# First four slots of an AdaLN and expert kernel written out, two pairs of blocks turned by TensorE, scatters set one by one among GpSimd's other work, and the last two pairs' scatters spaced by landings

## The reference, cut to what matters

```python
z = relu(hidden @ Wd[profile] + bd)              # 16 blocks of 256 rows x 256, a profile of 8 for each block
y = hidden + z @ Wu[profile] + bu
y = layernorm(y) * g[profile] + b[profile]
probs = softmax(y @ gate_w + gate_b)             # 8 experts
values, experts = top_k(probs, 2); values /= sum(values) + 1e-9
shared = gelu(y @ sh_w1 + sh_b1) @ sh_w2 + sh_b2                 # 256 -> 1024 -> 256
moe = sum over the two experts e of value_e * (gelu(y @ ew1[e] + eb1[e]) @ ew2[e] + eb2[e])
out = x + (y + shared + moe)
```

## Time and profile before

| | |
|---|---|
| median of 3 runs | 654.41 us (653.47 to 654.74) |
| the profiled execution's own time | 652.95 us, span 650.9 us |
| PE busy | 599.8 us, 92% of the span |
| DVE, ACT, POOL busy | 77%, 60%, 63% |
| first shared product / first expert product | 39.80 us / 243.46 us |

### The profile page before, as it was taken

One profiled execution on the slowest core, in us unless ns is written; L12 is line 12 of the kernel. 1 busy time (PEld: TensorE's weight loads), 2 busy tenths in 40 slices (PEclk: granted clock), 3 DMA queues, 4 the chain that ended last, 5 costly groups with the idle time before them and its releaser, 6 DMA issues.

```text
span 650.9 us, 16857 instructions
## 1 busy us (share of the span) xinstructions
PE 599.8 (92%) x5073; PEld 484.5 (74%) x5073; DVE 503.1 (77%) x1198; ACT 389.3 (60%) x662; POOL 413.1 (63%) x320
## 2 busy tenths in 40 slices
PE   4356999999989899999999999999999999999994
PEld 2223666766646668888888888888888888889883
DVE  3859889979975793898989898988896665656883
ACT  1638666667767774667675858576754444434641
POOL 2435687788887601285959585858688575756743
PEclk9768999999989999999999999999999999999998
DMA  7964467666144756367657585666686342424410
GB/s 265 304 145 133 128 190 151 215 195 154 57 126 121 247 160 191 84 125 134 147 105 155 126 142 130 137 133 129 90 71 73 52 73 44 67 41 59 69 26 3
DMA packets 116740, 81.31 MB, mean 125 GB/s; under 512 B 71090, under 2 KB 106162, under 8 KB 116658
## 3 DMA queue, kind: packets, MB, share of 16 engines
q1 hardware_dynamic: 101346, 61.16, 38.4%
q0 software_dynamic: 13296, 16.92, 15.3%
q10 hardware_dynamic: 2016, 2.16, 1.1%
HBM read 43.21 MB, written 24.42 MB: 104 GB/s over the span
## 4 chain that ended last, share of the span: by engine, by line
PE 71%; DVE 9%; issue 7%; POOL 4%; ACT 3%; DMA 3%; SPq 2%; POOLq 0%; ACTq 0%; DVEq 0%
PE H L1219 29%; PE Y L1235 29%; PE Y L1170 6%; PE H L1158 6%; SPq L287 2%; POOL xs_rows L430 2%; DVE wreg L768 1%; DMA xT<-wreg 1%; POOL wreg L413 1%; DVE wreg L737 1%; DMA wreg<-in_wpack 1%; DVE wreg L734 1%; DVE wreg L828 1%; ACT hf L554 1%; ACT wreg L501 1%
## 5 line engine op out<-in xcount | busy, mean ns | idle before, releaser
L608 ACT ACTIVATE hf<-H,prme 128x256 f32<-128x256 f32 (+1 forms) x312 | 151.0, 541 | 112.1 <-issue 97.4
L1219 PE MATMUL H<-xT,wreg 128*128 128x256 f16 (+1 forms) x1872 | 200.4, 263 | 0.2
L1235 PE MATMUL Y<-wreg,hh 128*128 x1136 | 188.6, 273 | 3.6 <-issue 2.4
L1219 PEld LDWEIGHTS H<-xT,wreg 128*128 x1872 | 171.9, 98 | 21.1 <-issue 0.7
L1235 PE MATMUL Y<-wreg,hl 128*128 x568 | 154.8, 273 | 0.0
L1235 PEld LDWEIGHTS Y<-wreg,hh 128*128 128x128 f16 x1136 | 111.0, 98 | 20.6 <-issue 6.1
L1031 DVE SCALAR_TENSOR_TENSOR hl<-hf,prme,hh 128x512 f16<-128x512 f32 (+1 forms) x156 | 115.1, 738 | 5.6
L1029 DVE TENSOR_SCALAR hh<-hf,prme 128x512 f16<-128x512 f32 (+1 forms) x156 | 84.6, 542 | 40.4 <-ACT hf L608 38.3
L457 POOL TENSOR_SCALAR b2w<-b2t,wsel 128x256 f32<-128x256 f32 x71 | 99.1, 1606 | 23.6 <-DMA b2t<-in_b 18.1
L1158 PE MATMUL H<-xT,wreg 128*128 128x512 f16 x384 | 93.8, 396 | 11.8 <-DMA xT<-wreg 11.7
L468 POOL DMA_INDIRECT out_y<-hh,xgm x36 | 64.7, 1799 | 58.0 <-DVE hh L1057 38.9
(11 more groups left out here) (189 smaller groups left out, 672.9 us busy)
## 6 DMA issues: line engine op xcount, KB each, us to landing
stage<-in_w SPq DMA_DIRECT2D x16, 1024.0 KB
b2t<-in_b SPq DMA_DIRECT2D x39, 128.0 KB
wreg<-in_wpack SPq DMA_DIRECT2D x16, 256.5 KB
wreg<-in_xt SPq DMA_DIRECT2D x16, 256.0 KB
wreg<-in_x SPq DMA_DIRECT2D x16, 256.0 KB, 5.6
wreg<-in_vecs SPq DMA_DIRECT2D x16, 256.0 KB, 4.0
out_y<-wreg SPq DMA_DIRECT2D x16, 256.0 KB, 2.2
xs_rows<-wreg SPq DMA_DIRECT2D x9, 260.0 KB
```

The costliest lines, as they stand in the source:

```text
L608: act.activation(hf[:, c, half * w:(half + 1) * w], H[c][:, half * w:(half + 1) * w], ACT.Gelu_apprx_tanh, bias=pr[:, ch:ch + 1], scale=pr ...
L1219: m = pe.matmul(H[c][:, half * w:(half + 1) * w], we[:, bass.ds(e + h * 2048 + k * 1024 + col, P)], xp[:, a + k, 0:w], start=i == 0, stop= ...
L1235: m = pe.matmul(Y[n % 2][:, j * D:(j + 1) * D], hx[:, n % 2, c * w + j * P:c * w + (j + 1) * P], we[:, bass.ds(e + 4096 + h * 2048 + c * D ...
```

## The change

Four things are done. **First slots.** Slots -7 to -1 leave the loops: each engine has their steps as straight code in another order, with other banks of PSUM for the first products (`z_of`, `u_of`, `MX0`), root and norm of pair 0 done block by block, and loads of more blocks started ahead. ScalarE's queue starts the 1 MB of unit 0 ahead of the four small vectors and takes over x of blocks 0 and 1. VectorE's `constants` stand ahead of the `v_xs` chain; `gate_halves`, the second block of pair 1 and unit 1 move behind slot 0. **Turning.** Pairs 0 and 1 (`PT` = 2) are turned by TensorE (`turn`, float32 products with the identity) into Y0 and Y1, and split from there by `high_turned` (ScalarE) and `low_turned` (VectorE). SP starts no transposes for them. **Zeros in waits.** `warm(n)` multiplies n times zeros by zeros, 14 times at the start and 6 times ahead of `turn(0)`. **Scatters.** Of pairs 0 to 5 single scatters stand between other GpSimd instructions. In pairs 6 and 7 each group of two waits until the group before it has landed.

```diff
+def turns(p):
+    return 16 * 4 * len(range(p % 3 + (3 if p % 3 < PT else 0), p + 1, 3))
...
+            load_shared(0)
             for dst, src in ((gnb_t[:, :], gnb.rearrange("t e (a c) -> (t e a) c", c=32)),
...
-            load_shared(0)
+            for b in range(2):
+                act.dma_start(acc_of(b), x[b].rearrange("(j p) d -> p j d", p=P)).then_inc(d_x[b], 16)
...
+            unit_sums(0)
+            relu(0)
+            relu(1)
+            load_shared(1)
+            unit_high(0)
+            relu(2)
+            norm(0, 0, 2)
+            norm(0, 2, 4)
+            high_turned(0)
+            high_turned(1)
+            relu(3)
+            high_rows(0)
+            unit_sums(1)
...
+            def turn(b):
+                pe.wait_ge(q_xn, b + 1)
...
+                for k in range(2):
+                    for j in range(2):
+                        t = pe.matmul(tn_of(b)[:, k, j * P:(j + 1) * P], yb_of(b)[:, j * D + k * P:j * D + (k + 1) * P], ident[:, :], start=True, stop=True)
+                t.then_inc(p_tn, 1)
...
+            def high_turned(b):
+                act.wait_ge(p_tn, b + 1)
+                act.wait_ge(v_xs, 1)
+                act.activation(xT16_of(b // 2)[:, 0:2, cols_of(b)], tn_of(b), ACT.Copy, scale=XS).then_inc(a_xt, 1)
...
+            def low_turned(b):
+                dve.wait_ge(a_xt, b + 1)
+                xp = xT16_of(b // 2)
+                dve.scalar_tensor_tensor(xp[:, 2:4, cols_of(b)], tn_of(b), XS, xp[:, 0:2, cols_of(b)], ALU.mult, ALU.subtract).then_inc(v_xt, 1)
...
+            def warm(n):
+                for i in range(n):
+                    pe.matmul(H[0][:, :], zpad[:, 0, 0:P], zpad[:, 0, 0:512], start=True, stop=True)
...
-                if c == 0:
-                    pe.wait_ge(d_tr[t % 3], 16 * 4 * (t // 3 + 1))
-                    if t == 0:
-                        pe.wait_ge(v_low, 1)
+                if c == 0 and t < PT:
+                    pe.wait_ge(v_xt, 2 * t + 2)
+                elif c == 0:
+                    pe.wait_ge(d_tr[t % 3], turns(t))
...
+            def scatter(p, i, q):
+                if (i, q) == (0, 0):
...
+                if p >= NP - 2 and q == 0 and i:
+                    pool.wait_ge(d_row[p % 3], 16 * (8 * (p // 3) + 2 * i))
+                elif p == NP - 2 and q == 0:
+                    pool.wait_ge(d_row[(p - 1) % 3], 16 * (8 * ((p - 1) // 3) + 7))
+                elif p == NP - 1 and q == 0:
+                    pool.wait_ge(d_row[(p - 1) % 3], 16 * 8 * ((p - 1) // 3 + 1))
```

More of the change, by code:

```diff
@@ L51 @@
 EARLY = 4
-START = [-6, -2, 27, 27]
+PT = 2
 PACE = 6
@@ L63, in upto, with seen @@
     return sum(blocks(k) for k in range(n))
-def early(s, d):
-    return [u for u in range(EARLY) if s == START[u] + d]
+def seen(p, hi):
+    return p + 1 + (p > 0 or hi == 4)
+def turns(p):
+    return 16 * 4 * len(range(p % 3 + (3 if p % 3 < PT else 0), p + 1, 3))
 def late(n, c, d):
@@ L339, in sync_program @@
             load_x(3)
-            for s in range(FIRST, NS):
+            load_xT(3)
+            load_adapter(3)
+            load_gb(2)
+            load_gb(3)
+            load_x(4)
+            load_x(5)
+            load_xT(4)
+            load_adapter(4)
+            load_xT(5)
+            load_adapter(5)
+            load_gb(4)
+            load_gb(5)
+            for s in range(NS):
                 if s == 26:
@@ L349, in sync_program @@
                 for p in at(s, -2):
[L350 to L353, removed]
+                    load_x(2 * p)
+                    load_x(2 * p + 1)
+                    for b in range(2 * p, 2 * p + 2):
                         load_xT(b)
@@ new lines, in even, with odd @@
+            def even(s, o, i, q):
+                for p in at(s, o):
+                    if p % 2 == 0 and p < NP - 2:
+                        scatter(p, i, q)
+            def odd(s, o, i, q):
+                for p in at(s, o):
+                    if p % 2 and p < NP - 2:
+                        scatter(p, i, q)
+            xb(0)
+            xb(1)
+            root(0, 0, 2)
+            root(0, 2, 4)
+            rows(0)
+            rows(1)
+            xb(2)
+            xb(3)
+            root(1)
@@ L974, in shared_rows @@
                 dve.scalar_tensor_tensor(a, Y[b % 2][:, :], pr[:, 10:11], a, ALU.mult, ALU.add).then_inc(v_acc, 1)
-            for s in range(FIRST, NS):
+            unit_scale(0)
+            variances(0, statistics(0), 0, 2)
+            variances(0, statistics(1), 2, 4)
+            roots(0, 0, 2)
+            roots(0, 2, 4)
+            gain(0)
+            gain(1)
+            unit_low(0)
+            low_turned(0)
+            low_turned(1)
+            statistics(2)
+            variances(1, statistics(3))
+            low_rows(0)
+            for s in range(NS):
                 t, q = s // 4, s % 4
@@ L997, in vector_program @@
                     choose(p)
-                if s == -1:
-                    gate_halves()
-                    constants()
-                if s < 4:
-                    for u in early(s, 4):
-                        unit_low(u)
-                if s < 4:
-                    for u in early(s, 2):
-                        unit_scale(u)
+                if s == 1:
+                    unit_scale(1)
                 if s == 28:
                     unit_scale(2)
-                if s >= 0:
-                    low_h(t, q)
+                low_h(t, q)
+                if s == 0:
+                    gate_halves()
+                if s == 2:
+                    low_turned(2)
+                    low_turned(3)
+                    unit_low(1)
                 if s == 27:
```

235 lines of the change are left out of this document (150 added, 85 removed).

## The result

The changed kernel takes **669.43 us** (median of 4 runs, 669.11 to 669.59); the kernel before, beside it, 654.4. The ratio is 1.0231 with a 95% interval of 1.0214 to 1.0249. The forecast was 643.3, so it was wrong by 26 us and in sign.

A forecast was written before the change was run, and what follows sets the result against it. TensorE was taken as short of work before 65 us and nearly full after. Start -9.6, single scatters -4.9 and spaced scatters +3.4 sum to -11.1, from 654.41 to 643.3 us; range 637 to 650.

The forecast's parts named there:

- the 14.5 gained ahead: Before the hand-over to the experts: gains of 9.6 us from the start and 4.9 from single scatters.
- The start: Up to the first `gemm2`: slot 0 11.6 us earlier, 2.0 given back, gain 9.6, between -1.7 and 16.2.
- Steps 1 and 2: Start: small vectors land at 9.5, 3.9 us late; the `v_xs` chain with `constants` then ends at 14.4.
- Step 3: Start: `unit_scale(0)`, statistics, root, norm and `gain` end at 23.7, the adapter's products fitting beside them.
- Step 4: Start: `unit_low(0)` takes 3.0 us and hides the turning; after two `low_turned` of 0.75 each, slot 0 starts at 28.2.
- given back in slots 0 to 3: VectorE's 7.4 us of moved work mostly fits 8.9 us of idle time; charged 2.0, between 0 and 7.4.
- Rival B: Late small vectors and work moved into slots 0 to 3 leave 4 to 5 of 9.6; 648 to 649; chance 0.17.
- D: VectorE's chain takes the start's gain, TensorE waiting at slots 5 to 22; about 654 us; chance 0.05.
- Single scatters: Scatters between GpSimd's instructions free VectorE; `low_rows(6)` 3.1 us earlier against slot 21; gain 4.9, bounds nothing to 5.8.
- Spaced scatters: Pairs 6 and 7: eight groups of 2.24 us plus landings of 2.76 delay the asking for rows; loss 3.4.
- Rival C: Spaced scatters take over the hand-over, landings of 5.6 us losing 26.1, deciding from 4.2; 666.0 us; chance 0.08.
- What the text said would show it wrong: Slot 0 after 33, the wait before slot 22 remaining, or the first expert product waiting over 5 us for rows.

The follow-up runs named there:

- e3: The changed kernel without the landing waits and with `gate_halves` between the two `low_turned` of the start; 658.28 us, ratio 1.0042 to the kernel before.
- e5: The changed kernel without landing waits, scatters of pairs 0 to 5 in runs as before, `gate_halves` between the two `low_turned`; 649.87 us, ratio 0.9924 to the kernel before.
- e9: e7 with `residual(0)`, `residual(1)` and `tokens(0)` ahead of `root(1)` in GpSimd's start; 646.84 us, ratio 0.99 to the kernel before.
- e6: The kernel before with only the scatters of pairs 0 to 5 placed singly, as in the changed kernel; 658.62 us, ratio 1.0062.
- e8: The same kernel as e4, run once more on another chip; 650.16 us in one execution.
- e2: The kernel before with only the landing waits added, pair 6's first waiting for all of pair 5; 669.38 us, ratio 1.0221.
- e4: The changed kernel without landing waits, with the scatters of pairs 0 to 5 in runs at their places before; 659.3 us, four executions.
- e7: e5 without the 14 and the 6 warming products of the start; 648.23 us, ratio 0.9902 to the kernel before.

## Why the prediction was wrong

Against its own time, the asking for rows was predicted at 243.1 less the 14.5 gained ahead, 228.6, and came at 255.35, 26.7 late; the time is 26.1 over. Three steps account for it.

**The start, predicted -9.6, is -2.5 at `gemm2` and -0.9 at slot 5.** Steps 1 and 2 held (the first reduce at 9.27, predicted 9.5). Step 3 was 1.7 short: `unit_low(0)` starts at 25.42, predicted 23.7. VectorE waited 1.11 us for `up` (`statistics` begins at 17.20, not 16.3), which the step had fitting beside it, and the second `gain` took 1.65 us in place of 0.7 beside `rows(0)`. Step 4 failed: it called the turning hidden behind `unit_low`. Here is VectorE, then GpSimd:

```profile
25.42 2.34 DVE L829 SCALAR_TENSOR_TENSOR wreg<-stage,sm,wreg 128x2048 f16<-128x2048 f32 x1
27.84 0.75 DVE L865 SCALAR_TENSOR_TENSOR xT<-Y,sm,xT 128x512 f16<-128x512 f32 x1
31.77 0.75 DVE L865 SCALAR_TENSOR_TENSOR xT<-Y,sm,xT 128x512 f16<-128x512 f32 x1 [3.18 <-ACT xT L587]
```

```profile
25.58 3.30 POOL L444 TENSOR_TENSOR wreg<-wreg 128x512 f32<-128x512 f32 x1 [0.63 <-DVE wreg L871]
```

`rows(1)` took 3.30 us beside `unit_low`, where `rows(0)` takes 1.26, and the turning of block 1, its copy and `low_turned(1)` are one chain behind it: 32.57 and not 28.2. The turning was also mis-sized, 2.0 us for both blocks: it took 2.08 and 2.07 a block, at the lower clock (0.50 from 25.0 to 32.5). The same exclusion that I had used for the scatters I left out here. Then "given back in slots 0 to 3", put at 2.0 of at most 7.4, came to 4.7 at `gemm2` (7.2 to 2.5) and 6.4 at slot 5. The idle time of 8.9 us that was to take the moved work did not help, because the work stood in the wrong places in VectorE's order: `gate_halves` behind slot 0's `low_h`, with `logits` of TensorE waiting 5.6 us (e3 and e5 show that moving it gives slot 2 back), and `roots(1)` beside `residual` (e9 shows 2.9 us at slot 3). Rival B, at half the gain, was nearer, and D, "VectorE's chain takes the start's gain", nearer still; I gave D 0.05. But D put the loss at slots 5 to 22, and it fell at slots 2 to 5.

**Single scatters, predicted -4.9, cost 6.2 from slot 5 to slot 21.** This step had the sign wrong. The row of 5.06 us was read rightly (VectorE stands behind a run of GpSimd's tensor instructions) and the run of three is indeed broken up. But it was the one bad case of 19, and I didn't ask what the other 18 had: before, 14 of them met no tensor instruction of 128 x 512 at all, and two more met one without being stretched. I also allowed for no loss: the bounds were "nothing" to 5.8 gained. The price by itself is +0.6% (e6). The step rested on `low_rows(6)` coming 3.1 us earlier against slot 21. It came 0.2 earlier: 0.59 us ahead of slot 21 before (176.01 and 176.60), 0.76 now (slot 21 at 181.93).

```profile
181.17 1.28 DVE L875 SCALAR_TENSOR_TENSOR wreg<-wreg,sm 128x1024 f16<-128x1024 f32 x1
```

```profile
188.97 0.21 PE L1252 MATMUL H<-wreg,xT 128*128 128x16 f16 x2 [1.67 <-DMA xT<-wreg]
```

The wait for `xT` ahead of slot 22 did shrink, from 3.17 us to 1.67, and the products behind it ran at the full clock, 1.00 in place of 0.75; together the difference falls from +5.3 at slot 21 to +2.2 at slot 23. Part of it is one of SP's four transposes, which takes 1.27 us to start in place of 2.03; the rest isn't shown. The 3 us were less than the loss ahead of them.

**Spaced scatters, predicted +3.4, cost 11.8.** The landing was sized right: from the end of each group to the next one, or to the asking, it is 1.7, 1.7, 5.5, 2.3, 4.4, 2.6, 1.8 and 2.3 us, 2.8 on average (2.76 predicted). Two terms were missing. One is the wait of 2.6 us of the first group for pair 5's landing. The other is that from there it took 45.9 and not 40.0 us, because the scatters themselves took 23.7 and not 17.9 us, 5.3 of it in two of pair 7 that took 4.49 and 2.74 us in place of 0.97, beside VectorE's `unit_low` and `low_h`. On the clock of the kernel before this is 203.07 + 2.6 + 45.9 = 251.6, which is 11.9 after 239.68; the predicted 3.4 and the missing 8.5. Rival C had the right side by the wrong lever: it asked for landings of 4.2 us, where these two terms made 11.9 at the predicted landing.

The two sums close: the first of these scatters stands at slot 25's clock, +3.9 where -14.5 was predicted, 18.4 us; with the 8.5 that is 26.9, against 26.7 found.

What the text said would show it wrong did: the first expert product waited 11.6 us, the wait before slot 22 was still there (1.67), and a `low_h` above 3 us (3.03) remained.

The parts on one scale, each alone against the kernel before of its own occasion: the start as changed -4.2 us (e8, one execution), single scatters +4.3 (e6), landing waits +13.3 (e2). They add up to +13.4, where the whole change measured +15.0; the 1.6 between them is about the width of the intervals. The start's part hangs on e8: the same kernel on the first chip, e4, was 3.2 us slower than the kernel before, with the stall.

## What to carry to other kernels

Where two engines exclude each other for whole instructions, count how many instructions of the one meet the other before a run is split: a run of long instructions hits one victim hard, and the same work spread out hits many. Moved work has to be placed where its engine waits anyway and ahead of whoever needs it; idle time summed over a window pays for nothing. A series of waits for landings is a serial chain of landing times, so add it from the time at which it really starts, without gains that aren't measured yet, and put every instruction between them at its longest.

## What the runs showed of the hardware

- A VectorE instruction on 128 x 4 values takes 0.16 us alone and 1.1 to 1.3 while a tensor instruction of GpSimd (1.26) runs: size doesn't protect it, it stands until the other is done. The Trainium skill (SBUF — State Buffer, "SBUF: two separate sides") calls it a lock held for an instruction, and the traces agree down to these, the smallest. It works in both directions: `rows(1)` took 3.30 us beside a 2.34 us instruction of VectorE.
- A scatter issued by GpSimd takes 0.97 us, and up to 6.83 (e2) beside VectorE's work. The 32 scatters over 1.2 us from 196 us to the hand-over, in twelve traces, end 0.83 to 0.86 us after a `low_h` (128 x 1024, 1.28 us) or a `unit_low` (128 x 2048, 2.33 us) of VectorE; a run of three such instructions without a gap holds one scatter for the whole of it.
- The landing of a group of two scatters of 128 rows, waited for on GpSimd or SP, took 1.7 to 5.5 us, 2.8 on average over the eight groups.
- One kernel ran at 659.3 us in four executions and at 650.2 in one on another chip. The profile of the first shows TensorE slowed to single products for 5 us, with no word in the chain of waits but "issue". The 16 KB transfer of instructions is 6.4 us later there (214.3 for 207.9), after TensorE had gone on. The cause stays open.
- Fourteen large products in the first microseconds did not keep TensorE's clock up: e5's four adapter products at 10.06 took 2.07 us, and e7's at 10.40, without them, 2.08; both take 1.02 at the full level.
